# Cross-attention with a routed expert layer: the rope products of k ahead of the normalisation of x on VectorE

## The reference

```python
q = layernorm(x) @ q_w.T + q_b;  k = ctx @ k_w.T + k_b;  v = ctx @ v_w.T + v_b
q = apply_rope(q) * d ** (-0.5);  k = apply_rope(k)   # x1*cos - x2*sin, x1*sin + x2*cos
...
x = x + softmax(windowed q.k) v @ o_w.T + o_b
logits = layernorm(x) @ router_w.T                    # top 2 of 8, capacity 1281 per expert
h = layernorm(x);  x = x + h + experts_of(h)
```

## Time and profile before

| | |
|---|---|
| runs of the kernel, median (lowest to highest) of 3 | 539.99 us (538.46 to 544.24) |
| profiled execution: its span, first to last instruction | 539.6 us |
| busy share of the span: PE, DVE, ACT, POOL | 76%, 63%, 49%, 61% |
| mean granted TensorE clock | 0.91 of full speed |
| first phase, about | 0 to 332 us |

### The profile page before, as it was taken

One profiled execution on the slowest core, in us unless ns is written; L12 is line 12 of the kernel. 1 busy time (PEld: TensorE's weight loads), 2 busy tenths in 40 slices (PEclk: granted clock), 3 DMA queues, 4 the chain that ended last, 5 costly groups with the idle time before them and its releaser, 6 DMA issues.

```text
span 539.6 us, 16107 instructions
## 1 busy us (share of the span) xinstructions
PE 408.6 (76%) x5587; PEld 318.6 (59%) x5587; DVE 341.9 (63%) x1062; ACT 263.8 (49%) x587; POOL 331.8 (61%) x282
## 2 busy tenths in 40 slices
PE   3463598888999999898988727799997988886100
PEld 2242476666777777676777613588886867665000
DVE  4785377888888788987877540477865545733200
ACT  1110355444665456565556520688896685764000
POOL 7442033377777777677765885038658786686683
PEclk9996799999999999999999968799999898989555
DMA  9997787588887887888895345346555454343331
GB/s 185 228 219 168 197 219 179 156 175 189 190 195 174 182 172 176 176 194 156 175 186 91 47 36 98 119 101 122 89 95 99 92 79 81 29 35 30 29 34 16
DMA packets 89045, 70.31 MB, mean 130 GB/s; under 512 B 8992, under 2 KB 75808, under 8 KB 88480
## 3 DMA queue, kind: packets, MB, share of 16 engines
q1 hardware_dynamic: 68208, 60.09, 43.8%
q0 software_dynamic: 20784, 9.53, 19.4%
HBM read 38.85 MB, written 30.74 MB: 129 GB/s over the span
## 4 chain that ended last, share of the span: by engine, by line
POOL 24%; issue 10%; PE 8%; DMA 8%; DVE 1%; SPq 1%; ACT 1%; POOLq 0%; DVEq 0%; ACTq 0%
POOL out L1421 16%; PE bank L470 7%; DMA out<-ys,row_token 6%; POOL queues L1332 5%; POOL base L1366 1%; PE bank L694 1%; DMA xs<-queues 1%; DMA queues<-rows,index 1%; SPq L354 0%; POOL parts L1395 0%; POOL rest L1392 0%; DMA q_pack<-maxT 0%; DVE ys L1229 0%; PE bank L725 0%; DVE xTp L1179 0%
## 5 line engine op out<-in xcount | busy, mean ns | idle before, releaser
L1421 POOL DMA_INDIRECT out<-ys,row_token x80 | 125.7, 1571 | 71.2 <-issue 47.9
L1332 POOL DMA_INDIRECT queues<-rows,index x64 | 100.0, 1562 | 19.2 <-issue 19.0
L918 DVE TENSOR_REDUCE maxima<-bank 128x4 f32<-128x512 f32 x128 | 87.2, 684 | 33.4 <-PE bank L470 31.6
L781 ACT ACTIVATE probs<-bank 128x512 f32<-128x512 f32 x128 | 76.4, 597 | 51.9 <-PE bank L470 51.2
L470 PE MATMUL bank<-xTp,w1p 128*128 128x512 f32 (+1 forms) x288 | 68.4, 391 | 10.2 <-DVE xTp L1179 10.2
L470 PE MATMUL bank<-k_pack,q_pack 128*64 128x128 bf16 x1024 | 54.4, 231 | 19.5 <-DMA k_pack<-k_scratch 17.7
L470 PEld LDWEIGHTS bank<-xTp,w1p 128*128 128x128 f32 x288 | 51.8, 207 | 20.7 <-DVE xTp L1179 12.3
L470 PE MATMUL bank<-q_pack,k_pack 128*128 128x64 bf16 x1024 | 52.6, 195 | 14.8 <-DMA q_pack<-maxT 14.2
L1287 DVE TENSOR_TENSOR hidp<-hid,hidp 128x512 fp32r<-128x512 f32 (+1 forms) x96 | 55.5, 600 | 13.2 <-ACT hidp L893 11.9
L470 PE MATMUL bank<-hidp,w2p 128*128 128x512 f32 (+1 forms) x288 | 62.3, 365 | 0.0
L889 ACT ACTIVATE hid<-bank 128x512 f32<-128x512 f32 (+1 forms) x96 | 53.0, 552 | 16.4 <-PE bank L470 16.2
(11 more groups left out here) (138 smaller groups left out, 677.1 us busy)
## 6 DMA issues: line engine op xcount, KB each, us to landing
k_pack<-k_scratch SPq DMA_DIRECT2D x64, 192.0 KB, 4.1
q_pack<-q_scratch SPq DMA_DIRECT2D x64, 128.0 KB, 3.2
queues<-empty SPq DMA_DIRECT2D x8, 682.5 KB, 7.4
xs<-queues SPq DMA_DIRECT2D x7, 650.0 KB
q_scratch<-parts SPq DMA_DIRECT2D x16, 192.0 KB
k_scratch<-parts SPq DMA_DIRECT2D x16, 192.0 KB
xin<-in_x SPq DMA_DIRECT2D x16, 128.0 KB, 3.4
cin<-in_ctx SPq DMA_DIRECT2D x16, 128.0 KB, 3.5
```

What stands on the lines that cost most here:

```text
L781: nc.scalar.activation(probs[u % 2][:], bb[u % 2][:], ACT.Exp).then_inc(S["prob_s"], 1)
L918: v.reduce_max(maxima[par][:, 4 * hg:4 * hg + 4, i2], ab[u % 2][:].rearrange("p (h c) -> p h c", c=P), AX).then_inc(S["max_s"], 1)
L1332: g.indirect_dma_start(queues, bass.IndirectOffsetOnAxis(ap=index[par][:, n:n + 1], axis=0), rows[par][:, n // TILES, n % TILES, :], None, ...
L1421: g.indirect_dma_start(out, bass.IndirectOffsetOnAxis(ap=row_token[par][0:n, t:t + 1], axis=0), ys[c][0:n, col // P, :], None, compute_op= ...
```

## The change

Part 3 of `norm1` moves behind the two products of k in DVE's order, in all steps but the first (k = -4), where the order stays. Nothing else changes: the instructions, their waits and the other engines' queues are the same.

```diff
                 maximum(k + 1, other, 5)
-                norm1(k, par, 3)
                 if isinstance(k, int) and k == FIRST:
+                    norm1(k, par, 3)
                     start()
                 rope(k, "roped_k", "k_mm", m2, 1, COSK, 2, 0)
                 rope(k, "roped_k", "k_mm", m2, 1, COSK, 2, 1)
+                if not (isinstance(k, int) and k == FIRST):
+                    norm1(k, par, 3)
                 if isinstance(k, int) and -3 <= k < -1:
                     masks(k + 3)
```

## The result

| | median (lowest to highest) | runs |
|---|---|---|
| before | 540.52 us (537.62 to 547.22) | 20 |
| after | 542.53 us (540.53 to 549.22) | 20 |
| after / before | 1.0055, 95% interval 1.0033 to 1.0076 | |

The change makes the kernel a little slower. The ratio is worth +3.0 us (1.8 to 4.1), the two medians lie 2.0 apart, and both are under the 1% that the forecast took as its border. The profiled execution of after spans 539.1 us, that of before 539.6: a single pair of spans can't show this difference, because the expert phase behind the change took anything from 203 to 208 us in the traces of these two kernels. So the stretches of the first phase are read instead.

The account below looks back on a forecast made before the run. No engine is full; a chain of waits, plain on POOL, sets the attention step at about 16.35 us. Loop +2.4, step 12 -0.5, start 0 sum to +1.9 us: 541.9 us, range 532 to 546.5.

Parts of the forecast that it names:

- What is removed: POOL's 1.56 us idle ahead of `qk` goes in each of eight steps, 12.5 us taken alone; PE's related waits go too.
- Who wins: At the end of `rstd1`, `qk` on POOL starts first and blocks `xn1` on DVE, which runs from 1.30 to 1.9 us.
- the first rival: DVE starts `xn1` ahead of `qk` and keeps its turn: period 15.4 us, eight steps -7.8, about 532.5 us; chance 0.22.
- The fall back by one instruction: DVE now loses to `qk`, `rest` and `parts`; POOL waits 2.0 us for `var2`, `rstd2` at 7.11 instead of 6.78.
- The term of +2.4 for the loop: Steps 4 to 11 of the attention phase: 0.3 us more in each of eight steps, +2.4 us.
- Given back at step 12: Step 12, without normalisation: PE's wait for maxima, about 0.9 us, is gone; half counted, -0.5 us.
- The start: Steps -3 to 3: late k products and `xn1` against `qk`, taken up by PE waits; zero, ends -1 to +2 us.
- Rival 2: Steps 0 to 4: POOL gets between the halves of `xn1`, maxima late, five times 1.3 us more, about 548 us; chance 0.14.
- Its floor of 15.42 us for SP: SP's issue work, 15.42 us from one write of the parts to the next, allows no shorter period.

Follow-up runs that it names:

- early-only kernel: The kernel before, with the changed order in steps -3 to 1 only and the old order from step 2 on: 540.93 us, ratio 1.001 (0.9976 to 1.0044).
- the two faster kernels: The changed kernel with `qk` also waiting for `xn1`: 536.96 us, ratio 0.995; and with the normalisation moved behind `var2` on DVE: 538.05 us, ratio 0.9941 to before.

## Why the prediction was right

The forecast was +1.9 us, 541.9 us, with most of the chance on a difference under 1%. Measured: a median of 542.53, +2.0 on the median of before in the same runs, and +3.0 (1.8 to 4.1) by the ratio. Its steps, each with the zero at the end of `rstd1` (219.03 in after):

- **What is removed.** k's products lie in DVE's idle stretch and `qk` follows `rstd1` directly, in seven of the eight steps: as forecast. PE's waits of rows 4 for `turned` and for the maxima read back are gone from these steps, or down to 0.2 us, as forecast; that PE then waits for DVE's maxima, up to 1.1 us, was not.
- **Who wins.** `qk` shuts `xn1` out, as forecast, against the first rival. One detail was off: the forecast let both halves of `xn1` follow `qk`, ending at 1.9. In fact the first half starts at 0.03, is held to 1.33, just behind `qk`, and `xn1` ends at 1.59. The next maximum so started at 1.51 instead of 1.81. That early 0.3 us bought nothing, since `over` was held to the end of `rest` either way.
- **The fall back by one instruction.** Forecast and measured: end of `over` 3.25 and 3.23, end of `index` 5.13 and 5.10, `var2` 6.85 and 6.81, `rstd2` 7.11 and 7.05, POOL's idle time 2.0 and 1.97, steps 16.6 and 16.63. This is the mechanism, and it holds. The term of +2.4 for the loop measured +2.0 from `qk` to `qk`, +2.2 from `rstd2` to `rstd2` (means of two traces each), but not as eight times 0.3: six steps (5 to 9 and 11) cost 0.26 to 0.29 each, step 4 gained 0.5, and step 10, with the low clock of PE that the forecast had not thought of, cost 1.0. That these two nearly cancel is luck.
- **Given back at step 12.** Forecast -0.5. From `rstd2` of step 11 to that of step 12 it is 14.14 in both traces of after, 15.00 and 15.09 before: -0.9. To the last scatter it is 74.15 and 75.48 against 76.25 and 77.18: -1.9. The sign was right, the size too small. In step 12 before, POOL waits 0.52 and 0.62 us for k's products in front of `qk`, and after it does not; what gives back the rest was not isolated.
- **The start.** Put at zero, with -1 to +2. The runs of the early-only kernel give -1.3 to +2.4 around +0.5. The two traces of each kernel put it at +1.7 (`rstd2` of step 3 at 123.92 and 126.71 before, 126.14 and 127.80 after), which is no more than the scatter of one kernel. Rival 2's mechanism is there (the rows of step 10 show it, and in steps -3 to 2 `xn1` is 1.56 to 1.58 long, `qk` between its halves), but its price, five times 1.3 us, is not.
- **The first rival** is a right sum for a case that does not come about by itself: the kernel in which `qk` waits for `xn1` forces it and has its 5.9 us from `rstd1` to `rstd2`. Its total of -7.8 us was too large (and 539.99 less 7.8 is 532.2, not 532.5); the runs gave -2.7. In every second step of the loop DVE's `diff` and `chosen` meet POOL's last scatter and `base` and make the products late, which the rival's working had not asked about. Its floor of 15.42 us for SP is none: after has 15.00.

So the mechanism in the loop was right and was tested. The total is right in part by luck: to the last scatter the traces give +1.9, made of +1.7, +2.2 and -1.9 where the forecast had 0, +2.4 and -0.5. The errors in the first and the last of these terms cancel, as far as two traces of each kernel can tell.

What stays open: what holds the two faster kernels at 16.0 and 16.1 us a step, with short steps of 15.3 to 15.6; why their tails, from step 11 on, are 1 to 2 us longer than before's; and why PE's clock falls in one step of after and not in the others.

## What to carry to other kernels

A wait can be what keeps two engines apart that disturb each other. Before taking one away, list which instructions will then be ready in the same instant, and look in the trace for rows of either engine whose lengths change with their neighbours; here 1.56 us a step were freed on POOL, 1.1 lost on DVE, and the step grew by 0.3. Where two such instructions meet, choose who goes first by what hangs on it: holding back `qk` for 0.72 us spared `xn1` 0.95 and gained 0.5% on the kernel before.

## What the runs showed of the hardware

Between queued instructions the two engines take uneven turns. Where POOL went from `rstd1` straight into the two halves of `qk`, DVE's waiting half of `xn1` got through only at the end of the second: 1.43 us for an instruction that takes 0.34 alone. In other steps of the same kernel, where `xn1` had begun first, its waiting second half got through between the two halves of `qk` (it ended at 152.78, they at 152.70 and 153.38). What decides between the two cases is not shown. POOL gets its turn as well: where `xn1` was first, `qk` ran between its halves although the second half was queued (after, step 10: `xn1` 236.18 to 237.74, `qk` 236.39 to 237.66). So with a `qk` in one piece either order cost `xn1` the same 1.56 us, and keeping the two apart in time, by a wait or by another place, brought 0.60 back.

The Trainium skill (SBUF — State Buffer, "Who interferes with whom") says that whichever of the two engines issues first holds the shared pair for its whole instruction and blocks the other. The rows agree as to a single instruction: the first half of `xn1`, started at 219.06 in after, ended at 220.36, 0.10 behind `qk`. Who goes next among queued instructions is told here by the runs alone.
